# Inverse deviations by ScalarE, a sixth state buffer, a ring of copies of C, and a new order of all steps in the main loop of a Mamba tower

## What is computed

```python
xz = layernorm(h) @ W_in;  x_inner, z = split(xz)
x_conv = silu(conv4(x_inner) + conv_b)
Bm, Cm = split(x_conv @ W_x)                      # 16 states each
delta = softplus(x_conv @ W_dt + b_dt)            # 384 channels
for t in sequence:
    hs = exp(delta_t * A) * hs + (delta_t * x_t) * B_t
    y_t = sum_over_states(hs * C_t)
out = ((y + D * x_conv) * silu(z)) @ W_out
h = h + (out - mean) * rsqrt(var + 1e-5) * gamma + beta
logits = layernorm(h) @ switch_w + switch_b       # then routing and experts
```

## Time and profile before

| | |
|---|---|
| median of 3 runs | 2832.25 us (2831.36 to 2832.88) |
| profiled execution, time | 2829.48 us |
| profiled execution, span | 2827.8 us |
| mean granted clock of TensorE | 0.928 of full |
| busy: TensorE, VectorE, ScalarE, GpSimd | 2487.8, 2256.8, 2061.3, 2269.8 us |
| VectorE scans, 768 | 1339.3 us |
| GpSimd products with C, 384 | 1247.6 us |
| ScalarE decays, 1536 | 838.8 us |

### The profile page before, as it was taken

One profiled execution on the slowest core, in us unless ns is written; L12 is line 12 of the kernel. 1 busy time (PEld: TensorE's weight loads), 2 busy tenths in 40 slices (PEclk: granted clock), 3 DMA queues, 4 the chain that ended last, 5 costly groups with the idle time before them and its releaser, 6 DMA issues.

```text
span 2827.8 us, 37925 instructions
## 1 busy us (share of the span) xinstructions
PE 2487.8 (88%) x12595; PEld 1562.7 (55%) x12595; DVE 2256.8 (80%) x2290; ACT 2061.3 (73%) x4512; POOL 2269.8 (80%) x1115
## 2 busy tenths in 40 slices
PE   7789888888989898888888989889886589999997
PEld 4445445454555554545454545455542278888886
DVE  2799999999999999999999999999999774222222
ACT  3688888888888888888888888888886463333432
POOL 0599999999999999999999999999998424544432
PEclk9898998989999999999989898999986599999999
DMA  3455544555554444555554455554444035666652
GB/s 105 115 128 119 129 115 112 126 119 131 118 116 112 112 112 112 129 128 121 128 118 112 112 131 120 128 118 112 112 95 95 18 121 202 223 207 215 214 182 89
DMA packets 165465, 361.08 MB, mean 128 GB/s; under 512 B 18353, under 2 KB 89593, under 8 KB 157848
## 3 DMA queue, kind: packets, MB, share of 16 engines
q1 hardware_dynamic: 152504, 329.59, 46.5%
q0 software_dynamic: 12768, 29.08, 3.2%
HBM read 293.86 MB, written 69.30 MB: 128 GB/s over the span
## 4 chain that ended last, share of the span: by engine, by line
PE 45%; DVE 23%; issue 12%; ACT 12%; POOL 7%; DMA 0%; DVEq 0%; POOLq 0%; SPq 0%; ACTq 0%
DVE arena L1528 13%; PE banks L1399 8%; DVE arena L1517 5%; PE banks L1378 5%; PE banks L1033 5%; PE banks L1072 5%; PE banks L1054 4%; PE banks L1104 4%; POOL arena L520 4%; PE banks L1116 3%; ACT banks L709 3%; PE banks L1386 3%; ACT arena L716 2%; POOL arena L609 2%; ACT L830 1%
## 5 line engine op out<-in xcount | busy, mean ns | idle before, releaser
L1528 DVE TENSOR_TENSOR_SCAN arena<-banks,arena 128x788 f32<-128x788 f32 x768 | 1339.3, 1784 | 61.2 <-ACT banks L709 31.0
L520 POOL TENSOR_TENSOR arena<-arena 128x1576 f32<-128x1576 f32 x384 | 1247.6, 3260 | 17.5 <-ACT arena L788 13.7
L709 ACT ACTIVATE banks<-arena,neg_a 128x392 f32<-128x392 f32 x1536 | 838.8, 580 | 247.2 <-DVE arena L1528 242.2
L1517 DVE TENSOR_TENSOR arena<-arena,banks 128x1576 f32<-128x1576 f32 x320 | 569.9, 1781 | 44.6 <-issue 33.1
L1104 PE MATMUL banks<-arena,gather_q 128*32 128x394 f32 x3072 | 354.8, 536 | 90.5 <-POOL arena L520 90.5
L1054 PE MATMUL banks<-arena,v_lo 128*128 128x394 f32 x768 | 311.5, 552 | 7.2 <-DVE logits L1547 4.4
L669 POOL DMA_INDIRECT out_tokens<-arena x114 | 115.0, 1009 | 244.0 <-DVE arena L1733 223.9
L1718 DVE TENSOR_TENSOR arena<-banks,arena 128x384 f32<-128x384 f32 x57 | 31.8, 558 | 347.4 <-PE banks L1399 347.4
L1072 PE MATMUL banks<-arena,wdt 128*128 128x394 f32 x576 | 246.1, 580 | 37.6 <-ACT arena L830 37.6
L1033 PE MATMUL banks<-wtok,arena 128*99 128x192 f32 x1536 | 266.3, 331 | 11.3 <-DMA arena<-in_x 11.3
L1033 PEld LDWEIGHTS banks<-wtok,arena 128*99 128x99 f32 x1536 | 249.4, 168 | 42.2 <-issue 33.0
(11 more groups left out here) (248 smaller groups left out, 4150.5 us busy)
## 6 DMA issues: line engine op xcount, KB each, us to landing
arena<-delta_du_scratch SPq DMA_DIRECT2D x384, 394.0 KB, 10.5
arena<-in_w_pack SPq DMA_DIRECT2D x57, 1155.0 KB, 5.3
delta_du_scratch<-arena SPq DMA_DIRECT2D x96, 394.0 KB, 3.3
arena<-in_x SPq DMA_DIRECT2D x32, 1176.0 KB, 12.3
rows_scratch<-arena SPq DMA_DIRECT2D x32, 297.0 KB
rows_scratch<-arena SPq DMA_DIRECT2D x32, 294.0 KB
arena<-in_b SPq DMA_DIRECT2D x57, 96.0 KB, 5.3
arena<-in_conv_w SPq DMA_DIRECT2D x1, 2304.0 KB, 11.1
```

Source lines behind the costliest of these rows:

```text
L520: pool.tensor_tensor(v[:, :, :], v[:, :, :], c_rep[r][:, u % NG].unsqueeze(1).to_broadcast([P, NQ, N2]), ALU.mult).then_inc(s_mulp, 1)
L709: ins = act.activation(o, d, ACT.Exp, scale=neg_a[:, c:c + 1])
L1517: dve.tensor_tensor(hb[(UNITS * n + u) % BUFS][:, :, :], rep[m][:, :, 1, :], ps_b[:, 0:N2].unsqueeze(1).to_broadcast([P, NQ, N2]), ALU.mul ...
L1528: dve.tensor_tensor_scan(v, decay[k % 2], v, 0.0, ALU.mult, ALU.add).then_inc(s_scan, 1)
```

## The change

Three kinds of edits. The inverse deviation is computed by ScalarE as exp(-0.5 ln(var + eps)), and GpSimd keeps only the product with the negated mean. There are six state buffers instead of five, and the copies of C lie in a ring of six instead of two sets of four. Every step of the four bodies gets a new place; the products with B stand a scan ahead of their own scan, the state sums are placed one by one instead of three units behind, and the table load is issued in iteration -1 too.

```diff
-BUFS = 5
-LAG = 3
+BUFS = 6
+CREPS = 6
+KEPT = (1,)
-        c_rep = [carve(P, NG, N2) for _ in range(2)]
+        c_rep = [carve(P, N2) for _ in range(CREPS)]
...
-            def rstd_front(n):
+            def centre_front(n):
                 need(pool, s_hn, n)
-                pool.wait_ge(s_var[0], n + 1)
-                pool.tensor_tensor(rs1[:, :], var1[:, :], small[0:H0, 0, :], ALU.pow).then_inc(s_pow[0], 1)
                 pool.wait_ge(s_pow[0], n + 1)
                 pool.tensor_tensor(nb1[:, :], neg1[:, :], rs1[:, :], ALU.mult).then_inc(s_rs1, 1)
...
             def front_deviation(n):
                 act.wait_ge(s_sq1, n + 1)
-                act.activation(var1[:, :], sq1[:, :], ACT.Identity, scale=1.0 / DIM, bias=eps[0:H0, 0:1]).then_inc(s_var[0], 1)
+                act.activation(var1[:, :], sq1[:, :], ACT.Ln, scale=1.0 / DIM, bias=eps[0:H0, 0:1]).then_inc(s_var[0], 1)
+                act.wait_ge(s_var[0], n + 1)
+                need(act, s_hn, n)
+                act.activation(rs1[:, :], var1[:, :], ACT.Exp, scale=-0.5).then_inc(s_pow[0], 1)
...
             def copy_c(n, r, o, g):
                 act.wait_ge(s_cb, NG * n + g + 1)
-                need(act, s_mulp, UNITS * (n - 1))
-                act.activation(c_rep[r][:, g], kbank(CS[g], o)[:, 0:N2], ACT.Copy).then_inc(s_cc, 1)
+                need(act, s_mulp, c_uses(NG * n + g - CREPS))
+                act.activation(c_rep[(NG * n + g) % CREPS], kbank(CS[g], o)[:, 0:N2], ACT.Copy).then_inc(s_cc, 1)
...
             def spread_b(n, r, u):
                 if u == 0:
                     pe.wait_ge(s_bc3, n + 1)
-                need(pe, s_bx, bx_count(n, u))
-                if u == KEEP + 1:
-                    pe.wait_ge(s_bkeep, n + 1)
+                p = SPREAD[SPREAD.index(u) - 1]
+                m = n if u != SPREAD[0] else n - 1
+                if p not in BY_POOL:
+                    need(pe, s_bx, bx_count(m, p) + 1)
+                if p in KEPT:
+                    need(pe, s_bkeep, len(KEPT) * m + KEPT.index(p) + 1)
...
```

More of the change, by code:

```diff
@@ L56 @@
 UNITS = MB * NG
-KEEP = 1
 BY_POOL = (5, 9)
+KEPT = (1,)
 BXS = UNITS - len(BY_POOL)
-BUFS = 5
-LAG = 3
+SPREAD = tuple(u for u in range(UNITS) if u not in BY_POOL or u in KEPT)
+BUFS = 6
 REP = 16 * SP
@@ L74, in need @@
 def need(eng, sem, count):
-    if not isinstance(count, int) or count > 0:
+    if count > 0:
         eng.wait_ge(sem, count)
@@ L391, in bx_count, with c_uses, spread_count, kept_copy @@
             return BXS * n + u - sum(1 for b in BY_POOL if b < u)
+        def c_uses(j):
+            return UNITS * (j // NG) + UNITS - NG + j % NG + 1
+        def spread_count(n, u):
+            return len(SPREAD) * n + SPREAD.index(u)
+        def kept_copy(u):
+            return [v % NG for v in KEPT].index(u % NG)
         def hidden_part(g, f):
@@ L614, in body @@
                     if -2 in on and u == 0:
[L615 to L629, removed]
+                        centre_rows(i - 2)
                     if 0 in on and u > 0:
@@ L757, in row_deviation @@
                 act.activation(mv3[:, :, 0], mv3[:, :, 0], ACT.Copy, scale=-1.0)
-                act.activation(mv3[:, :, 1], mv3[:, :, 1], ACT.Identity, bias=eps[0:H0, 0:1]).then_inc(s_var[2], 1)
+                act.activation(mv3[:, :, 1], mv3[:, :, 1], ACT.Ln, bias=eps[0:H0, 0:1]).then_inc(s_var[2], 1)
+                act.wait_ge(s_var[2], n + 1)
+                need(act, s_rows, n)
+                act.activation(rs3[:, :], mv3[:, :, 1], ACT.Exp, scale=-0.5).then_inc(s_pow[2], 1)
             def out_deviation(n):
@@ L762, in out_deviation @@
                 need(act, s_rs2, n)
-                act.activation(var2[:, :], sq2[:, :], ACT.Identity, scale=1.0 / DIM, bias=eps[0:H0, 0:1]).then_inc(s_var2, 1)
+                act.activation(var2[:, :], sq2[:, :], ACT.Ln, scale=1.0 / DIM, bias=eps[0:H0, 0:1]).then_inc(s_var2, 1)
+                act.wait_ge(s_var2, n + 1)
+                need(act, s_onorm, n)
+                act.activation(rs2[:, :], var2[:, :], ACT.Exp, scale=-0.5).then_inc(s_rs2, 1)
             def out_norm(n):
@@ L786, in copy_c, with keep_b @@
                 act.wait_ge(s_cb, NG * n + g + 1)
-                need(act, s_mulp, UNITS * (n - 1))
-                act.activation(c_rep[r][:, g], kbank(CS[g], o)[:, 0:N2], ACT.Copy).then_inc(s_cc, 1)
[L790 to L793, removed]
+                need(act, s_mulp, c_uses(NG * n + g - CREPS))
+                act.activation(c_rep[(NG * n + g) % CREPS], kbank(CS[g], o)[:, 0:N2], ACT.Copy).then_inc(s_cc, 1)
+            def keep_b(n, j):
+                u = KEPT[j]
+                act.wait_ge(s_bb, spread_count(n, u) + 1)
+                if u not in BY_POOL:
+                    act.wait_ge(s_bx, bx_count(n, u) + 1)
+                need(act, s_bxp, len(BY_POOL) * (n - 1) + max(
+                    p for p, v in enumerate(BY_POOL, 1) if kept_copy(v) == j))
+                act.activation(b_keep[j], ps_b[:, 0:N2], ACT.Copy).then_inc(s_bkeep, 1)
             def copy_product(n, r, o, t):
@@ L943, in body @@
                         copy_front_t(i + 2, r, 1)
+                    if -1 in on and k == 21:
+                        out_deviation(i - 1)
                     if -1 in on and k == 21:
@@ L1179, in body @@
                         spread_c(i, r, r, 3)
-                    if 1 in on and u == 2:
+                    if -1 in on and u == 2:
+                        state_sum(i - 1, o, 11)
+                    if 0 in on and u == 2:
+                        spread_b(i, r, 3)
+                    if 0 in on and u == 3:
+                        state_sum(i, r, 0)
+                    if 1 in on and u == 3:
                         if 0 in on:
@@ L1313, in _ @@
                         for b in range(2):
+                            need(pe, s_trf_copied, b)
                             front_t(0, 0, b, True)
@@ L1609, in body @@
                 for k in range(2 * UNITS):
-                    if 0 in on:
-                        if k % 2 == 0 and k // 2 not in BY_POOL:
-                            bx(i, k // 2)
-                        scan(i, k)
+                    if 0 in on and k == 0:
+                        bx(i, 0)
                     if -2 in on and k == 0:
                         row_stats(i - 2, r)
-                    if -1 in on and k == 5:
+                    if 0 in on:
+                        scan(i, k)
+                    if 0 in on and k == 0:
+                        bx(i, 1)
+                    if 0 in on and k == 3:
+                        bx(i, 2)
+                    if -1 in on and k == 3:
                         if i == PAIRS:
@@ L1637, in body @@
                         take_logits(i - 2, r)
+                    if 0 in on and k == 21:
+                        bx(i, 11)
+                    if 0 in on and k == 21:
+                        take_y(i, r, 1)
             for i in range(-2, PAIRS + 2):
```

327 lines of the change are left out of this document (183 added, 144 removed).

## The result

The changed kernel takes 2715.2 us (2714.24 to 2718.85, 4 runs) against 2832.03 us (2831.36 to 2832.88, 4 runs): a ratio of 0.959, 95% interval 0.9573 to 0.9606. The forecast was 2757 us with a range from 2720 to 2806 us.

The account below looks back on a forecast made before the run. VectorE and GpSimd, both full, plus TensorE clock stalls were taken as the bound. Floor 62.4, interlocks 0.5 and clock 1.2 gave 64.1 us an iteration; with the ends, 75.6 us saved: 2757 us, range 2720 to 2806.

Parts of the forecast that it names:

- What bounds the kernel: Main loop, kernel before: VectorE and GpSimd both full, some 2 us of each 66.37 us iteration stalls with TensorE's slow clock.
- two neighbours of the earlier trace: Two adjacent main-loop iterations of the kernel before, 64.45 and 66.22 us, read as showing what an iteration is made of.
- a floor of 62.4 us: VectorE's time an iteration without stalls, forecast to fall from 64.1 us with products with B a scan ahead.
- the ten hops: VectorE: each scan starting right after its own product costs 0.16 to 0.18 us; ten an iteration, 1.7 us.
- The rival on tables: ScalarE: each small Ln and Exp pair reloads tables, six loads of 1.28 us, 65 us; about 2830 us, chance 0.03.
- clock losses and interlocks: Main loop, above VectorE's floor: 0.5 us an iteration for engines' interlocks and 1.2 us for TensorE's slow clock.
- The halving of today's loss: Main loop: clock losses of 2.3 us an iteration taken to fall to 1.2 us, pauses being shorter.
- The walk: New order stepped through with old durations over one iteration: TensorE's pauses at most 1.2 us, states finished in time.
- the clean rival: Main loop: no slow TensorE stretch remains; 62.9 us an iteration, 2722 us in all, chance 0.20.
- The tight place: TensorE around the router: convolution 0, state sum 8, then unit 0's spread; slack 0.2 us at full rate.
- The ends: Outside the 28 iterations: prologue saves 3 us, drain 5 us, three first and last iteration 4 us together.
- the saving forecast there: Drain: Ln and Exp for powers on the chain and the residual ahead of the last states save 5 us.

Follow-up runs that it names:

- e9: Kernel before plus 64 extra matmuls an iteration of no use, ahead of four state sums' waits, adding to unused columns without the start flag: 2771.86 us, ratio 0.9794.
- e10: Kernel before with Ln and Exp on ScalarE for GpSimd's three powers, plus 64 extra matmuls an iteration: 2768.24 us, ratio 0.9781.
- e12: Changed kernel with the spread for unit 0 ahead of state sum 8 and 26 extra matmuls an iteration: 2702.66 us, ratio 0.955.
- e1: Kernel before with only Ln and Exp on ScalarE for GpSimd's three powers, and the table load in iteration -1: 2872.33 us, ratio 1.0151.
- e2: Kernel before with only VectorE's products with B moved a scan ahead and row statistics ahead of scan 0: 3191.41 us, ratio 1.1271.
- e5: Changed kernel with only VectorE's products with B put back directly ahead of their own scans: 3168.73 us, ratio 1.1216.
- e13: Changed kernel with the three powers back on GpSimd and 26 extra matmuls an iteration, on another chip: 2844.93 us, ratio 0.9948.
- e8: Kernel before plus 64 extra matmuls an iteration with the start flag, ahead of four state sums' waits; part of the sums lost: 2771.84 us, ratio 0.9796.

## Why the prediction was right and wrong

*What bounds the kernel.* Right. Two full engines, and 2 us an iteration of slow clock with its consequences: e9 gives 64.36 us at full rate and 2.0 us for the rest, where 64.1 and 2.3 were read from the rows. But the two neighbours of the earlier trace rows are not the usual pair. An iteration of 64.4 us comes only three times in 28; the others mostly alternate like these of the kernel before:

```profile
616.55:683.53 66.98, 59.72 (x310) 32.96 (x309) 63.09 (x56) 56.62 (x121) 64.11 (x28) 1.00 0.52 118
683.53:749.67 66.14, 59.03 (x275) 33.88 (x276) 63.23 (x56) 56.68 (x121) 63.31 (x28) 0.87 0.54 124
```

The longer one is at full rate: the slow stretch ends one iteration, and VectorE's wait for it opens the next. Two smaller slips: the earlier trace rows has 14 waits for the row deviation, not 13, and 39 waits for decays in 26 iterations are not once in two.

*VectorE.* Right in kind and size: a floor of 62.4 us was forecast from the spacing in the earlier trace rows, and the quick iterations take 62.22 us. e10 against e12 bears the ten hops out, 1.8 us.

*GpSimd.* 60.4 us busy forecast, 60.95 measured in the quick iteration; over the 28 the mean fell from 63.7 to 60.9. That it stops being an equal bound is right. What the forecast had no term for is what e1 shows: in the old order that relief makes the kernel slower, through the clock.

*ScalarE.* The small instructions cost 0.3 us for an Ln and 0.2 for an Exp, as the groups of the quick iteration show for the front deviation:

```profile
L736 ACT ACTIVATE arena<-arena,small 99x4 f32<-99x4 f32 x1 | 0.3, 295 | 0.0
...
L739 ACT ACTIVATE arena<-arena 99x4 f32<-99x4 f32 x1 | 0.2, 205 | 0.0
```

ScalarE is busy for 56.90 us, less than the 57.5 forecast. No table load came with them: there are two an iteration, as before. (The rival on tables had a slip in its sum: at 65 us an iteration, by the same sum as the others, it would end near 2787 us, not 2830.)

*The failed step: clock losses and interlocks.* The sum had 0.5 us for interlocks and 1.2 us for the clock, 1.7 us an iteration. Measured are 62.60 − 62.22 = 0.38 us, and VectorE's waits in these 28 iterations make 0.36 of them. Over 28 iterations the difference is 37 us, and the floor 0.2 us lower is another 5; these are the 42 us by which the forecast missed. (The ends gave 9.3 us for the 12 forecast, and the medians lie 2.1 us further apart than the two profiled spans.) The mechanism was right, the size of this term was not. The halving of today's loss was a choice with nothing measured behind it. The walk said more: it had TensorE's pauses at 1.2 us at most and less waiting in both light stretches, and that should have moved weight to the clean rival, which asked for 62.9 us. The walk's interlocks were paper ones: in the whole loop VectorE waits 3.6 us at other places than those 12.

*The tight place.* Right. Nearly the only stall left is the one named, convolution 0, state sum 8 and the spread for unit 0, and it comes once in three iterations with 0.6 to 1.0 us in the 28, not up to 5.7, because the slow stretch there lasts some 3.5 us. In the kernel before it was 10, as a window of that kernel shows:

```profile
1337.00:1347.00 10.00, 9.22 (x37) 5.66 (x36) 9.79 (x8) 8.48 (x20) 10.00 (x6) 0.50 1.04 208
```

There TensorE ran at the lower level, 0.50 of full rate, over the sum, the router and most of convolution 0.

*The ends.* The three first and the last iteration gave 4.5 us for 4 forecast, and the prologue 2.1 for 3, but the latter by luck: the cause given is not the one. The loads ahead of the first Exp and Ln did go:

```profile
57.00 1.28 ACT L700 ACT_TABLE_LOAD   x1
...
66.15 1.19 ACT L855 ACTIVATE arena<-arena 128x1182 f32<-128x1182 f32 x1
...
88.55 2.12 ACT L713 ACTIVATE banks<-arena,neg_a 128x392 f32<-128x392 f32 x4 [1.06 <-DMA arena<-delta_du_scratch]
```

That shortens the softplus by 2.7 us, but the delta products before it come later and at a lower clock (7.89 us instead of 6.20), so its last step ends at 70.86 us instead of 69.91. The first decays, which wait for the copies of delta, start at 88.55 instead of 90.32 us all the same; why the copies land sooner no run shows. Nor do they set the time of the first product with B. That waits for the spread of unit 0, and so for a convolution, first in the kernel before and then in the changed one:

```profile
87.21 4.81 PE L1054 MATMUL banks<-arena,v_lo 128*128 128x394 f32 x8 [1.32 <-ACT arena L783]
...
93.18 0.33 PE L1088 MATMUL banks<-arena,pick 128*128 128x394 bf16 x1
```

```profile
87.08 2.88 PE L1072 MATMUL banks<-arena,v_lo 128*128 128x394 f32 x8 [1.07 <-ACT arena L796]
...
91.12 0.33 PE L1109 MATMUL banks<-arena,pick 128*128 128x394 bf16 x1
```

The convolution ran at a granted clock of 0.59 before and of 1.00 now: 1.9 of the 2.1 us.

In the drain it was 2.7 for 5. GpSimd's timeline shows a part of why, against the earlier trace rows:

```profile
2074.08 2.98 POOL L533 TENSOR_TENSOR arena<-arena 128x1576 f32<-128x1576 f32 x1 [4.27 <-PE banks L1125]
...
2088.84 1.82 POOL L548 TENSOR_TENSOR arena<-arena,gam 99x768 f32<-99x768 f32 x1 [2.14 <-ACT arena L781]
...
2099.06 3.25 POOL L525 TENSOR_TENSOR arena<-arena 128x1576 f32<-128x1576 f32 x1
```

It is held up in the last iteration by a sum and by the output norm, and so it still finishes the last unit 7.7 us after the last scan (9.3 before); the saving forecast there took it to be free by then. Another 0.9 us come from the power that went from the second normalisation. The power of the output norm gave nothing, as from the last unit to the product with gamma it is 13.8 us in both kernels: the output product of the last pair takes 6.53 us instead of 5.49, and four of ScalarE's copies now stand ahead of that deviation.

*Two rules against the traces.* The Trainium skill (TensorE: Matmul & The Clock Gate, Part 1) says that activity releases the throttled state. e9 agrees, with 1.00 instead of 0.94 in the loop. The strict reading, that only an idle engine falls back, is not borne out by e1, where TensorE is busy for 91% of the window at 0.89 and no wait of its matmuls is longer than 1.4 us (430 to 2100 us). The switch of 2.66 us that the Trainium skill gives (ScalarE: Activation LUTs, What ACT_TABLE_LOAD costs) didn't come into play: no load was added to the loop.

## What to carry to other kernels

Where several engines run fixed lists at over 90%, a step's place on one list and its consumer's place on another are one edit: here moving only one of the two cost 12% (e2, e5), both together gained 4%. Before pricing a stall, look whether TensorE's matmuls take twice as long there; if they do, a few matmuls of no use in its pauses can both show the cause and remove it (e9, e10). Check that they raise the clock: in e13 they did not, and the run decided nothing. A producer directly ahead of its reader on one in-order engine costs a hop that a neighbour's independent work can fill.

## What the runs showed of the hardware

Relieving an engine lowered TensorE's clock: the mean over 430 to 2050 us is 0.94 in the kernel before, 0.89 in e1 with 68.3 us an iteration, and 1.00 in e10, which is e1 with 64 small matmuls more an iteration, with 64.35. And e8 against e9: a matmul with the start flag into columns 394 to 511 of a PSUM bank spoiled sums that were being accumulated in columns 0 to 393 of that bank; without the flag it didn't, and the time was the same.
